# A mixture-of-experts patch convolution: four images' patches side by side in K = 97 rows, read lot by lot into a ring

## The reference

```python
xn = (x - mean) / sqrt(var + eps)                       # per image and channel
patched = patchify(pad(xn), 8)                          # (32*25, 32, 10, 10)
logits = patched.mean(axis=(2, 3)) @ Wg + bg            # 8 experts
routing = one_hot(argmax(logits)) * softmax(logits)
outs = relu(conv3x3(patched, Wexp[e]) + bexp[e])        # every expert
y = x + unpatchify(sum_e routing[:, e] * outs[e])
```

## Time and profile before

| | us |
|---|---|
| median of 3 runs | 221.12 |
| lowest, highest | 217.77, 224.03 |
| the profiled execution's own time | 215.9 |
| its span, first to last instruction | 213.8 |

### The profile page before, as it was taken

The page is one execution under the profiler, slowest core; times in us unless marked ns, Lnnn a source line. Parts: engine busy times, 40 slices in busy tenths (PEclk is TensorE's granted clock), DMA queues, the critical chain, the costliest instruction groups (busy, mean ns, idle before and its releaser), DMA issues.

```text
span 213.8 us, 11088 instructions
## 1 busy us (share of the span) xinstructions
PE 113.7 (53%) x4880; PEld 104.7 (49%) x4880; DVE 139.9 (65%) x273; ACT 81.7 (38%) x242; POOL 79.1 (37%) x207
## 2 busy tenths in 40 slices
PE   0000308666179637476559746745767759466620
PEld 0000308656179527365458646635656658455620
DVE  3889793336992589564995699367946990383145
ACT  2391349009600591019502940096006900650000
POOL 8489429109400580019201920094006800670000
PEclk9999999889956996789575896799585875988995
DMA  6868997962499577996499478987499869902002
GB/s 225 325 269 200 272 342 179 240 167 96 168 288 246 172 304 173 242 265 223 168 289 264 137 295 209 239 235 249 157 286 261 317 154 229 285 22 101 6 3 98
DMA packets 82415, 44.91 MB, mean 210 GB/s; under 512 B 77888, under 2 KB 78016, under 8 KB 81344
## 3 DMA queue, kind: packets, MB, share of 16 engines
q1 hardware_dynamic: 81792, 43.21, 72.0%
q10 hardware_dynamic: 576, 1.00, 1.3%
HBM read 29.77 MB, written 14.43 MB: 207 GB/s over the span
## 4 chain that ended last, share of the span: by engine, by line
PE 44%; issue 24%; DVE 17%; ACT 5%; ACTq 4%; DMA 2%; POOLq 2%; POOL 0%; DVEq 0%
PE conv_bank L395 38%; DVE SUMS L216 5%; ACT WIND L325 4%; ACTq L101 3%; PE pick_bank L383 3%; DVE NEWT L202 2%; DVE PROD L221 2%; DMA XT<-x 2%; PE logit_bank L374 2%; DVE XN L210 2%; POOLq L101 2%; DVE GATE L223 1%; DVE BLK L263 1%; PE pick_bank L385 1%; DVE BLK L268 1%
## 5 line engine op out<-in xcount | busy, mean ns | idle before, releaser
L395 PE MATMUL conv_bank<-XG,WS 128*32 128x64 f32 x4800 | 103.3, 256 | 62.3 <-issue 56.4
L395 PEld LDWEIGHTS conv_bank<-XG,WS 128*32 128x32 f32 x4800 | 94.2, 134 | 69.0 <-issue 68.8
L165 POOL COPY WS<-WP 128x192 f32 x200 | 60.1, 353 | 107.1 <-issue 93.5
L335 ACT COPY WS<-WP 128x192 f32 x200 | 52.1, 348 | 51.3 <-issue 43.7
L257 DVE STREAM_TRANSPOSE YT<-conv_bank 128x320 f32<-128x320 f32 x40 | 19.1, 499 | 16.6 <-PE conv_bank L395 16.6
L216 DVE TENSOR_REDUCE SUMS<-WIND 128x25 f32<-128x2500 f32 x8 | 22.1, 2759 | 10.9 <-ACT WIND L325 10.8
L245 DVE TENSOR_SCALAR IDX<-pick_bank 1x57 int32<-1x57 f32 x8 | 1.7, 206 | 29.3 <-PE pick_bank L385 29.3
L374 PE MATMUL logit_bank<-GATE,CONST 128*100 128x8 f32 x32 | 5.4, 278 | 26.8 <-DVE GATE L223 26.8
L325 ACT COPY WIND<-XN 128x2500 f32<-128x2500 f32 x8 | 18.8, 2350 | 1.7 <-DVE XN L210 1.7
L374 PEld LDWEIGHTS logit_bank<-GATE,CONST 128*100 128x100 f32 x32 | 4.7, 221 | 27.8 <-issue 21.9
L263 DVE STREAM_TRANSPOSE BLK<-YT 128x1024 f32<-128x1024 f32 x8 | 16.8, 2100 | 0.1
(11 more groups left out here) (28 smaller groups left out, 54.3 us busy)
## 6 DMA issues: line engine op xcount, KB each, us to landing
XG<-windows SPq DMA_DIRECT2D x24, 1000.0 KB, 10.1
windows<-WIND SPq DMA_DIRECT2D x8, 1250.0 KB, 5.1
XT<-x SPq DMA_DIRECT2D x8, 512.0 KB, 4.4
out<-XT SPq DMA_DIRECT2D x16, 256.0 KB, 4.5
CONST<-consts ACTq DMA_DIRECT2D x1, 390.0 KB, 4.6
BLK<-wtab ACTq DMA_DIRECT2D x1, 384.0 KB, 9.5
WGS<-wgs ACTq DMA_DIRECT2D x1, 200.0 KB, 6.2
BG<-bg ACTq DMA_DIRECT2D x1, 4.0 KB, 8.1
```

The source lines that it names most:

```text
L165: last = nc.gpsimd.tensor_copy(WS[:, at % RING, ACT_PAIRS + i, :], WP[:, bass.ds(index[lot * POOL_PAIRS + i], PAIR)])
L335: last = nc.scalar.copy(WS[:, at % RING, i, :], WP[:, bass.ds(index[lot * ACT_PAIRS + i], PAIR)])
L395: last = nc.tensor.matmul(o, WS[:, at % RING, n % LOT * 2 + b // 2, column:column + C], taps, start=kx == 0, stop=kx == TAPS - 1)
```

## The change

The K rows of the convolution go from 128 to 97 (3 shifts by 32 rows, and one row of ones at the end). WP, WS and XG have 97 partitions. The DRAM tensor of windows has the four images of a group side by side in each row (row 32 n + j holds 4 by 100 elements), so it is written by one DMA for each image with runs of 400 B (3,200 in all for a group), and read with runs of 380 elements (1,520 B), lot by lot: three DMAs of 160 runs. XG is a ring of eight lots. For group 0 the writes are split: channels 0 to 6 of each image first (7 partitions, enough for lot 0), then channels 7 to 31 (25 partitions), two images by SP and two by ACT. PE waits for the taps of each lot.

The normalisation moves to ACT (`normalise`, Identity with scale and bias NEGMR, which DVE makes in `deviation`). The gate's sums come from XN by row sums over ten lines (4 strips of 34 columns, 1,360 elements), one copy for the last strip and a sum of ten columns (250 elements), and so need `normalised`, not `windows_ready`. `logits(g+2)` is issued behind lot 3 of g, `picks(g+1)` behind lot 0; at the start PE issues `logits(1)` ahead of the first convolution. The probability map has 16 elements and is made by POOL (`spread`); `finish` turns into patch order, applies relu and probability by one instruction, and adds by four strips. Index registers are loaded for each lot, five at a time. The table comes by the first DMA on ACT's queue, with 97 rows, and is laid in 16 pieces of 768 elements: 12 by POOL and 4 by ACT, ACT's ahead of `root(0)`. The memsets of XG are gone; the ones come by a DMA. x has five buffers.

The diff, cut:

```diff
-XB = 4
+XB = 5
+KP = TAPS * C + 1
+RX = 8
+FIRST = -(-LOT * C // NP)
+SPAN = GI * WIN * WIN
+READ = SPAN - WIN * WIN + PS * WIN
+ACT_LAYS = 4
...
-        XG = [sb(f"XG{u}", [128, GN, KROWS]) for u in range(2)]
-        WS = sb("WS", [128, RING, PAIRS, PAIR])
-        WP = sb("WP", [128, E * E * PAIR])
+        XG = sb("XG", [KP, RX * LOT, SPAN])
+        WS = sb("WS", [KP, RING, PAIRS, PAIR])
+        WP = sb("WP", [KP, E * E * PAIR])
...
+        def window_rows(u, b, first, last):
+            return windows_dram[u][first * NP:last * NP, b * WIN * WIN:(b + 1) * WIN * WIN
+                                   ].rearrange("(c k) w -> c k w", k=NP)
+        def window_tile(b, first, last):
+            return WIND[b * C + first:b * C + last].rearrange("c (k w) -> c k w", k=NP)
...
-                sp.dma_start(windows_dram[u].rearrange("(p k) w -> p (k w)", k=NP), WIND[:]
-                             ).then_inc(windows_written, 16)
+                for b in range(GI):
+                    sp.dma_start(window_rows(g % 2, b, 0, C), window_tile(b, 0, C)).then_inc(windows_written, 16)
+            def load_taps(g, lot):
+                at = g * LOTS + lot
+                source = windows_dram[g % 2].rearrange("(n j) w -> j n w", j=C)[:, lot * LOT:(lot + 1) * LOT]
                 for ky in range(TAPS):
+                    rows = bass.AP(XG, (ky * RX + at % RX) * LOT * SPAN,
+                                   [[TAPS * RX * LOT * SPAN, C], [SPAN, LOT], [1, READ]])
+                    sp.dma_start(rows, source[:, :, ky * WIN:ky * WIN + READ]).then_inc(taps_loaded[at % RX], 16)
+            def read_lot(g, lot):
+                at = g * LOTS + lot
+                sp.wait_ge(windows_written, 16 * GI * (g + 1))
+                if at >= RX:
+                    sp.wait_ge(conv_done, at - RX + 1)
+                load_taps(g, lot)
...
+            sp.wait_ge(windows_ready, 1)
+            for b in range(GI):
+                sp.dma_start(window_rows(0, b, 0, FIRST), window_tile(b, 0, FIRST)).then_inc(first_written, 16)
+            for b in range(GI // 2):
+                sp.dma_start(window_rows(0, b, FIRST, C), window_tile(b, FIRST, C)).then_inc(windows_written, 16)
+            sp.wait_ge(first_written, 16 * GI)
+            load_taps(0, 0)
+            for lot in range(1, LOTS):
+                read_lot(0, lot)
             write_windows(1)
+            read_lot(1, 0)
+            read_lot(1, 1)
...
-            nc.gpsimd.memset(XG[0][:], 1.0).then_inc(ones_set, 1)
             pool.wait_ge(table_loaded, 16)
-            nc.gpsimd.tensor_copy(bass.AP(WP, 0, [[E * E * PAIR, 128], [E * PAIR, E], [PAIR, E], [1, NW]]),
-            nc.gpsimd.memset(XG[1][:], 1.0).then_inc(ones_set, 1)
+            for e in range(E):
+                lay_even(e)
+            for e in range(ACT_LAYS, E):
+                last = lay_odd(e)
+            last.then_inc(pairs_laid, 1)
...
-                dve.wait_ge(windows_ready, g + 1)
-                nc.vector.tensor_reduce(SUMS[:], WIND[:].rearrange("p (k w) -> p k w", k=NP),
-                                        AX.X, ALU.add).then_inc(sums_ready, 1)
+                dve.wait_ge(normalised, g + 1)
+                nc.vector.tensor_reduce(
+                    bass.AP(ROWSUM, 0, [[NB * PITCH, 128], [PITCH, KEEP], [1, W + 2]]),
+                    bass.AP(XN, 0, [[PITCH * PITCH, 128], [PS * PITCH, KEEP], [1, W + 2], [PITCH, WIN]]),
+                    AX.X, ALU.add)
...
             statistics(0)
             deviation(0)
-            normalise(0)
-            statistics(1)
-            deviation(1)
             dve.wait_ge(small_loaded, 16 * 3)
             gate(0)
-            normalise(1)
+            statistics(1)
             routing(0)
+            probability(0)
             selection(0)
+            deviation(1)
             gate(1)
...
+            act.dma_start(WT, wtab).then_inc(table_loaded, 16)
             act.dma_start(CONST[:], consts).then_inc(small_loaded, 16)
...
-            act.dma_start(WT, wtab).then_inc(table_loaded, 16)
             nc.scalar.preload_act_table_set("natural_log_exp_and_others")
+            act.wait_ge(table_loaded, 16)
+            for e in range(ACT_LAYS):
+                last = lay_odd(e)
+            last.then_inc(pairs_laid, 1)
             root(0)
+            normalise(0)
             windows(0)
+            for b in range(GI // 2, GI):
+                act.dma_start(window_rows(0, b, FIRST, C), window_tile(b, FIRST, C)).then_inc(windows_written, 16)
             root(1)
             exponent(0)
+            copies(0, 0)
+            copies(0, 1)
+            normalise(1)
+            windows(1)
+            copies(0, 2)
+            copies(0, 3)
...
             logits(0)
             picks(0)
+            logits(1)
+            pe.wait_ge(ones_loaded, 16)
             for g in range(GROUPS):
-                pe.wait_ge(taps_loaded[g % 2], 16 * TAPS * (g // 2 + 1))
                 for lot in range(LOTS):
                     at = g * LOTS + lot
+                    pe.wait_ge(taps_loaded[at % RX], 16 * TAPS * (at // RX + 1))
...
                     if lot == 0 and g + 1 < GROUPS:
-                        logits(g + 1)
-                    if lot == 2 and g + 1 < GROUPS:
                         picks(g + 1)
+                    if lot == 3 and g + 2 < GROUPS:
+                        logits(g + 2)
```

More of the change, by code:

```diff
@@ L33, with build @@
 RING = 5
-C_OWN, C_CODE, C_SPAN, C_HOME, C_PAIR, C_END = 0, 256, 264, 520, 720, 780
-def build(nc, x, wgs, bg, wtab, consts, out):
+SPREAD = KEEP * KEEP
+C_OWN, C_CODE, C_SPAN, C_HOME, C_PAIR, C_END = 0, 256, 264, 296, 496, 556
+def build(nc, x, wgs, bg, wtab, ones, consts, out):
     fp32, i32 = mybir.dt.float32, mybir.dt.int32
@@ L176, in _ @@
                 pool.wait_ge(index_ready, g + 1)
-                index = pick_rows(pool, g, POOL_AT, LOTS * POOL_PAIRS)
                 for lot in range(LOTS):
-                    copies(g, lot, index)
+                    copies(g, lot)
+                    if lot == 1:
+                        spread(g)
         @block.vector
@@ L290, in _ @@
                     statistics(g + 2)
+                if g + 1 < GROUPS:
+                    routing(g + 1)
+                if g + 2 < GROUPS:
+                    deviation(g + 2)
+                if g + 1 < GROUPS:
+                    probability(g + 1)
                 if g > 0:
+                    turn_lot(g - 1, LOTS - 1)
                     finish(g - 1)
                 if g + 1 < GROUPS:
-                    routing(g + 1)
+                    selection(g + 1)
                 turn_lot(g, 0)
-                if g + 1 < GROUPS:
-                    selection(g + 1)
+                turn_lot(g, 1)
                 if g + 2 < GROUPS:
-                    deviation(g + 2)
-                    normalise(g + 2)
-                for lot in range(1, LOTS):
-                    turn_lot(g, lot)
-                    if lot == 3 and g + 2 < GROUPS:
-                        gate(g + 2)
+                    gate(g + 2)
+                turn_lot(g, 2)
+                turn_lot(g, 3)
+            turn_lot(GROUPS - 1, LOTS - 1)
             finish(GROUPS - 1)
@@ L314, in root, with normalise @@
                 nc.scalar.activation(ROOT[:], LN[:], ACT.Exp, scale=-0.5).then_inc(root_ready, 1)
+            def normalise(g):
+                act.wait_ge(rstd_ready, g + 1)
+                if g > 0:
+                    act.wait_ge(windows_ready, g)
+                    act.wait_ge(sums_ready, g)
+                inside = bass.AP(XN, PITCH + 1, [[PITCH * PITCH, 128], [PITCH, H], [1, W]])
+                nc.scalar.activation(inside, XT[g % XB][:].rearrange("p (h w) -> p h w", w=W), ACT.Identity,
+                                     bias=NEGMR[:], scale=RSTD[:]).then_inc(normalised, 1)
             def exponent(g):
-                act.wait_ge(centred, g + 1)
+                act.wait_ge(below_max, g + 1)
                 nc.scalar.activation(LEXP[0:GN], LMINUS[0:GN], ACT.Exp, accum_out=LSUM[0:GN]).then_inc(exp_done, 1)
@@ L328, in windows, with copies @@
                 ).then_inc(windows_ready, 1)
-            def copies(g, lot, index):
+            def copies(g, lot):
                 at = g * LOTS + lot
+                index = pick_rows(act, g, lot * ACT_PAIRS, ACT_PAIRS)
                 if at >= RING:
@@ L350, in _ @@
             exponent(0)
-            windows(1)
             act.wait_ge(pairs_laid, 2)
             act.wait_ge(index_ready, 1)
-            index = pick_rows(act, 0, 0, LOTS * ACT_PAIRS)
-            for lot in range(LOTS):
-                copies(0, lot, index)
-            for g in range(GROUPS - 1):
+            copies(0, 0)
[4 more added lines that the diff above has]
+            copies(0, 3)
+            for g in range(GROUPS):
                 if g + 2 < GROUPS:
@@ L359, in _ @@
                     root(g + 2)
-                exponent(g + 1)
-                act.wait_ge(index_ready, g + 2)
```

(15 more changed lines are left out.)

182 lines of the change are left out of this document (104 added, 78 removed).

## The result

The changed kernel takes 270.28 us (median of 4 runs, 269.23 to 274.24); the kernel before, on the same chip, 219.59 us (4 runs). The ratio is 1.239, with a 95% interval of 1.231 to 1.247. The forecast was 228 us with a range of 208 to 236. The direction was right; the size was wrong by 42 us.

A forecast was written before the change was run, and what follows sets the result against it. PE's waits for blocks of its own program were taken as the bound. Table 22, start 24.7, lot 1's taps 1, middle 165 and end 7.6 gave 220.3 us of span, 228 us on the median's scale; whole range 208 to 236.

The forecast's parts named there:

- What bounds the kernel: PE stops at the end of each block of its own program until the next block is there.
- T: Start: time at which the table has landed; 5.3 us if spread over engines, 22.4 if one engine carries it; 22 taken.
- The start behind it: Start: nine steps from the table's landing until PE begins, together 24.7 us.
- Steps 1, 4 and 8, and 6 and 7 together: Start: ACT's table pieces 2.7 us, normalisation 1.0, registers and copies for two lots 4.0; statistics(1) 1.9, routing to indices 2.75.
- The middle: Convolutions: 173.3 us less 4.9 of gate waits and 3 of late program blocks, 165 us (155 to 173).
- third rival: Table late, middle gives nothing back: dear rows or late taps, middle 173, start + 6, 234 to 236 us; chance 0.12.
- Cover: Middle: changes in DVE, ACT and POOL work cost nothing, since PE's queue covers them.
- The gate waits: Middle: PE's waits for DVE's gate sums go, saving 4.9 us.
- The end: After the convolutions: four strips by one instruction save about 0.3 us; 7.6 us.
- early table: Rival at the start: 97 rows spread like 128, table lands at 5.3 us, time 210 us; chance 0.28.
- Late but free: Rival: table late, but spread lots let program blocks through; middle 155, time 217 us; chance 0.12.
- DMA shares near 1.0 throughout: Sign in the new profile, named as one that would show the forecast wrong; no size given.

The follow-up runs named there:

- e4: Changed kernel without most of its window writes from group 2 on and most reads behind the first eight lots; 217.52 us (one run).
- e1: Changed kernel with the 97-row table loaded by two transfers, of 96 rows and 1 row; 250.49 us, 1.152 of the kernel before.
- e2: e1 with the table and the taps filled up to 128 rows (zero weights); 245.52 us, 1.127 of the kernel before.
- r10: e2 with tap rows put back at partitions 4j + ky in place of 3j + ky, XG filled with ones at the start; 228.15 us.
- e3: Kernel before with its convolution matmuls over only the first 97 of 128 rows; 218.31 us, 1.005 of the kernel before.
- r13: r10 without most of its window writes from group 2 on; 212.81 us (one run).
- e6: e1 without most of its window writes from group 2 on, reads kept; 233.15 us (one run).
- r12: Old DRAM side, 4j + ky taps, 128 rows; the change's row sums, ACT normalisation, earlier gate, table in pieces; group 0 read by 24 transfers; 218.44 us.
- r15: r12 with group 0's patches read by three transfers in place of 24; 214.23 us, 0.988 of the kernel before.
- e5: e1 with the kernel before's DRAM side: windows written in 10,000 B rows, patches read in 9,600 rows of 320 B; 242.98 us, 1.116 of the kernel before.
- r14: r10 with the reads of a group's five lots issued together at the start of the group before; 229.9 us, 1.052 of the kernel before.
- r9: Kernel before with tap rows at partitions 3j + ky in place of 4j + ky, its table laid to match; 241.33 us.

## Why the prediction was wrong

*What bounds the kernel* held. All but two of PE's stops in the changed kernel's middle and start that the profile names "issue" are for its own program blocks, and these grow with the data traffic. The Trainium skill ("Runtime: NRT & Kernel Launch", section "Instruction fetch mechanics") calls the fetch of the next 16 KB mostly hidden. The traces disagree: about 39 us of such stops are left even in e4 (43.5 less waits of 2.5 and 1.9 for taps and weights), about 57 in the changed kernel (60.9 less 2.2 and 1.9).

*T, the table's landing*: 22 forecast, 21.5 measured. The choice of the high end was right, and e1 shows that the shape of the transfer was the reason.

*The start behind it*: 24.7 forecast, 30.0 measured (21.5 to 51.5). The row sums were priced at 1.10 ns for each of 1,360 elements, 1.5 us; they took 2.64, and two gates stand on the path: 2.3 us. Then PE waited 2.24 us for the taps of lot 0. These had no term in the sum at all; I had priced only those of lot 1. `WIND` was ready at 31.53, but SP issued six writes, up to 4.6 us each, before it issued the first read at 43.30, and the third read of lot 0 landed at 51.41, T + 29.9. In e1 it is the same: landed at 35.93, PE at 36.02. The rest are tenths. Steps 1, 4 and 8, and 6 and 7 together, came out within 0.7 us each. Lot 1 did not wait for its taps (1 forecast).

*The middle*: 165 forecast, 208.1 measured. This is the step that failed, in three ways.

- The row of 1,520 B was taken at 64 ns, nearer to the large rows; it took 99.3. The bound that I had written beside it, from the small rows' rate, was 104. Of the 35 ns, 20.1 are the partition stride (98.1 in e2, 78.0 in r10), which I did not see in the diff at all: I wrote of "97 rows in place of 128" only that numbers and columns stay.
- The row of 400 B was taken at 17 to 27 ns and took 34.5.
- With these a group needs 2,400 x 99.3 / 16 = 14.9 us, 6.9 and 2.8 us for x and out: 24.6, against my 16 to 18. Eight groups are 197 us, which is more than the whole middle of before. Even my own high bounds gave 15.6 + 5.4 + 2.8 = 23.8 us a group, 190 in eight. I priced the third rival, "the middle gives nothing back", at 173 with them, as though the middle could not grow. So the range ended at 236 although its own bounds reached further. Even the third rival's sum falls short of its own terms: 8 us in the middle and 6 at the start on top of 220.3 are 234.3 of span, and on the scale of the medians, on which the other forecasts stand, about 242.

*Cover*: that DVE, ACT and POOL cost nothing in the middle held but for the 1.88 us at 73.47, when PE waited for ACT's copies. That the matmuls stay the same did not hold as written (134.8 us against 103.3), but hardly cost anything (e3: 0.5%), because the time was taken from the stops.

*The gate waits* (4.9 us) went, as forecast. *The end* took 7.8 for 7.6.

*The rivals*: the early table fell at T. "Late but free" fell with the middle. "Nothing back" named the right mechanism with a chance of 0.12 and a price of 8 us; it was 43. The signs I had named as those of an error, "DMA shares near 1.0 throughout", are what the trace shows.

How the middle follows the work can now be read from the table. With 128 rows, r13, r10 and e2 (130.3, 166.2, 194.5 us of work) have middles of 168.9, 187.5 and 202.6: 0.52 us for each us of work. With 97 rows, e4, e6 and e1 (61.5, 151.5, 197.6) have 156.5, 187.4 and 206.2: 0.34 and 0.41. So the DMA engines were not the only bound, and yet a us of their work had a price of a third to a half within one form of the kernel. Between forms this does not carry over: before, r12 and r15 have the same work (153.8 to 154.3) and middles of 173.3, 178.6 and 167.6, and e5 has more work than e1 and a shorter middle.

## What to carry to other kernels

Where an engine stops for blocks of its own program and these stops grow with the data traffic, price the DMA work of a stage as a cost on the path (here a third to a half of it) even if no engine waits for data, and carry the upper bound of a row's price through to the end of the range. Look at the partitions in which a transfer's rows lie, not only at their number and length: a packed layout that saves a quarter of the partitions cost 22 to 24 us of 217. A table of 97 rows was worth a second, tiny transfer (e1). And when a reordered run gives the same time, look at its waits before calling the order harmless: in r14 two of them had changed by 16 and 17 us in opposite directions.

## What the runs showed that I had not expected

- The partition stride of a read: 32.1 ns for a row of 320 B at stride 3 and 21.8 at stride 4 (r9, before); 98.1 and 78.0 ns for 1,520 B (e2, r10).
- The granted clock changes with the matmuls' rows, but not with them alone. With the same order of work, 97 rows for 128 brought the mean granted clock from 0.835 to 0.721 (before, e3), and 128 for 97 from 0.646 to 0.806 (e1, e2). Yet at 97 rows it also rises when there is little traffic and the stops are short: from 100 to 140 us it was 0.54 in e1 and 0.74 in e4. The stretch from 60 to 100 us, in before and then in e3:

```profile
60.00:100.00 40.00, 25.45 (x1124) 23.61 (x1117) 25.49 (x61) 14.17 (x42) 11.65 (x41) 0.81 0.86 230
```

```profile
60.00:100.00 40.00, 34.67 (x1111) 32.35 (x1106) 27.28 (x61) 15.79 (x48) 13.28 (x45) 0.50 0.84 225
```

- The transfer of 97 rows also held up what its queue issues behind it: CONST's issue took 5.75 us behind the table, 0.46 us behind a table of 128 rows (r15).
- The clock column prints full speed until the first clock record. In the changed kernel that is at 111 us, and its mean of 0.746 is too high; the blocks of 3.64 us before that time are at the lower level.
